# Strassen weight sums made by accumulating DMAs from GpSimd's queue in place of VectorE additions

## What is computed

```python
def lora_add(base, inp, A, B):                 # one A, B pair per sequence, rank 16, scale 0.5
    return base + einsum('bor,bnr->bno', B, einsum('bri,bni->bnr', A, inp)) * 0.5

# block 1: W_gate, W_up (1376, 512), W_down (512, 1376)
act  = silu(lora_add(x @ W_gate.T)) * lora_add(x @ W_up.T)
y    = lora_add(act @ W_down.T)
# block 2: RMS norm of y, gate_w, up_w (1792, 512), down_w (512, 1792)
nx   = y * rsqrt(mean(y * y) + 1e-5) * ln_w
out  = x + (silu(nx @ gate_w.T) * (nx @ up_w.T)) @ down_w.T
```

## Time and profile before

| | us |
|---|---|
| median of 3 runs | 397.09 (396.99 to 397.59) |
| span of the profiled execution | 395.5 |
| TensorE busy (matmuls) | 391.8 |
| VectorE busy | 314.8 |
| ScalarE busy | 240.8 |
| GpSimd busy | 10.6 |
| HBM read | 29.95 MB |

### The profile page before, as it was taken

One profiled execution on the slowest core, in us unless ns is written; L12 is line 12 of the kernel. 1 busy time (PEld: TensorE's weight loads), 2 busy tenths in 40 slices (PEclk: granted clock), 3 DMA queues, 4 the chain that ended last, 5 costly groups with the idle time before them and its releaser, 6 DMA issues.

```text
span 395.5 us, 5733 instructions
## 1 busy us (share of the span) xinstructions
PE 391.8 (99%) x1984; PEld 327.3 (83%) x1984; DVE 314.8 (80%) x476; ACT 240.8 (61%) x386; POOL 10.6 (3%) x13
## 2 busy tenths in 40 slices
PE   9999999999999999999999999999999999999997
PEld 5899888888888888888888888888888888888885
DVE  4899979586835869578699787878787869899994
ACT  5969786857574469815745656464646494484740
POOL 6300000000000000000000000000000000000000
PEclk9999999999999999999999999999999999999999
DMA  7640243311111551000400021313130316105112
GB/s 271 182 133 0 83 133 98 110 53 55 53 55 54 164 154 57 2 0 0 159 2 1 12 97 55 106 53 108 60 119 37 89 57 199 55 1 201 54 53 108
DMA packets 14942, 32.42 MB, mean 82 GB/s; under 512 B 2370, under 2 KB 4930, under 8 KB 14914
## 3 DMA queue, kind: packets, MB, share of 16 engines
q1 hardware_dynamic: 13792, 30.22, 23.7%
q10 hardware_dynamic: 1122, 1.84, 1.3%
HBM read 29.95 MB, written 2.10 MB: 81 GB/s over the span
## 4 chain that ended last, share of the span: by engine, by line
PE 99%; DVE 0%; issue 0%; DVEq 0%
PE bank L1365 53%; PE bank L1705 17%; PE bank L1593 14%; PE bank L1511 3%; PE bank L1557 3%; PE bank L1546 3%; PE bank L1375 3%; PE bank L1615 1%; PE bank L1607 1%; PE bank L1505 1%; PE bank L1714 0%; PE bank L1622 0%; DVE act L1354 0%; DVEq L1352 0%
## 5 line engine op out<-in xcount | busy, mean ns | idle before, releaser
L1365 PE MATMUL bank<-xs,ws 128*128 128x512 f32 x840 | 195.0, 390 | 0.0
L1365 PEld LDWEIGHTS bank<-xs,ws 128*128 128x128 f32 x840 | 156.6, 188 | 31.9
L415 ACT ACTIVATE xs<-act 128x512 fp32r<-128x512 f32 x71 | 42.8, 623 | 21.1 <-DVE act L1045 7.6
L1593 PE MATMUL bank<-xs,wdc 128*128 128x512 f32 x240 | 55.7, 390 | 0.0
L1593 PEld LDWEIGHTS bank<-xs,wdc 128*128 128x128 f32 x240 | 44.8, 188 | 9.5 <-issue 0.2
L889 DVE TENSOR_TENSOR xs<-act,xs 128x512 fp32r<-128x512 f32 x71 | 47.5, 685 | 2.7 <-ACT xs L415 2.1
L889 DVE TENSOR_TENSOR ws<-wraw,ws 128x256 fp32r<-128x256 f32 (+2 forms) x45 | 30.0, 668 | 13.0 <-ACT ws L415 12.8
L415 ACT ACTIVATE bank<-bank 128x512 f32<-128x512 f32 x30 | 17.3, 580 | 34.5 <-PE bank L1365 33.7
L415 ACT ACTIVATE mu<-bank 128x512 f32<-128x512 f32 x44 | 26.1, 596 | 20.1 <-PE bank L1365 13.6
L1705 PE MATMUL bank<-xs,vs 128*128 128x512 f32 x168 | 38.2, 389 | 0.0
L1705 PEld LDWEIGHTS bank<-xs,vs 128*128 128x128 f32 x168 | 31.5, 188 | 6.5
(11 more groups left out here) (133 smaller groups left out, 439.5 us busy)
## 6 DMA issues: line engine op xcount, KB each, us to landing
wraw<-wgu_in SPq DMA_DIRECT2D x22, 512.0 KB, 3.3
wdr<-vs_in SPq DMA_DIRECT2D x7, 512.0 KB, 3.6
wraw<-vj_in SPq DMA_DIRECT2D x3, 896.0 KB, 4.7
wdr<-wd_in SPq DMA_DIRECT2D x10, 256.0 KB, 2.7
xa<-xT_in SPq DMA_DIRECT2D x4, 256.0 KB, 4.1
xa<-xT_in ACTq DMA_DIRECT2D x2, 512.0 KB, 4.7
bgu_raw<-bgu_in SPq DMA_DIRECT2D x32, 32.0 KB, 1.9
xres<-xT_in SPq DMA_DIRECT2D x4, 256.0 KB, 3.5
```

The source lines that it names most:

```text
L415: return nc.scalar.activation(out_ap, in_ap, ACT.Copy, scale=scale)
L1365: ins = mm(z[:, :], w_slot(j)[:, w, s, k * P:(k + 1) * P], xs[:, c, r, k, :], start=(start and k == 0 and s == 0 and r == 0), stop=(k == 1 ...
L1593: ins = mm(z[:, :], wd[:, s, h * P:(h + 1) * P], x[r], start=(start and s == 0 and r == 0), stop=False, skip_group_check=True)
```

## The change

The host hands over the raw blocks of each weight set three times: `wgu_in` holds the three blocks that are split as they are (384 KB a set), `wbase_in` four blocks with which the sums begin (512 KB), and `wmore_in` three blocks that are added to the first three of these (384 KB). SyncE loads the first into `wraw` and the second straight into `wsum`, which has two buffers now. GpSimd then issues two DMAs that add to their destination: `wmore_in` onto blocks 0 to 2, and, when that has landed, block 1 onto blocks 2 and 3. `wraw` and `wsum` become parts of one tensor, `wbuf`; the order of two sums in the weight slot is swapped; the mask lies in memory that was free at that time; the zeroing of `ad` stands behind the sums of set 9. Steps 1, 3 and 4 above keep their places and waits, but for the semaphore on which `hi_b` waits.

```diff
-W11, W12, W22, WS3, WS1, WS2, WS4 = range(7)
+W11, W12, W22, WS3, WS1, WS4, WS2 = range(7)
...
-        mask = sb("mask", [P, CH], f32)
...
-        wraw = sb("wraw", [P, 2, 4, 256], f32)
-        wsum = sb("wsum", [P, 4, 256], f32)
+        wbuf = sb("wbuf", [P, 14, 256], f32)
...
             raw1 = sb("bgu_raw1", [P, 4, CHUNK[1]], f32, way)
+            sb("skip_ad", [P, 64], f32, way)
+            mask = sb("mask", [P, CH], f32, way)
...
-        w0_raw = wraw[:, :, :, :].rearrange("p a b n -> p (a b n)").rearrange("p (k x) -> p k x", k=KT)
+        wraw = wbuf[:, 0:6, :].rearrange("p (a b) n -> p a b n", a=2)
+        wsum = wbuf[:, 6:14, :].rearrange("p (a b) n -> p a b n", a=2)
+        w0_raw = wbuf[:, 6:14, :].rearrange("p b n -> p (b n)").rearrange("p (k x) -> p k x", k=KT)
...
-        jraw = wraw[:, :, :, :].rearrange("p a b n -> p (a b) n")
-        dm5 = wsum[:, :, :].rearrange("p a n -> p (a n)").rearrange("p (i n) -> p i n", i=2)
+        jraw = wbuf[:, 0:KF, :]
+        dm5 = wbuf[:, 10:14, :].rearrange("p a n -> p (a n)").rearrange("p (i n) -> p i n", i=2)
...
-                sp.dma_start(wraw[:, j % 2, :, :], wgu_in[j - 2].rearrange("p (a m) -> p a m", a=4)
+                sp.dma_start(wraw[:, j % 2, :, :], wgu_in[j - 2].rearrange("p (a m) -> p a m", a=3)
                              ).then_inc(s_w_ld[j % 2], 16)
+                sp.dma_start(wsum[:, j % 2, :, :], wbase_in[j - 2].rearrange("p (a m) -> p a m", a=4)
+                             ).then_inc(s_wbase_ld[j % 2], 16)
...
-            pool.wait_ge(s_stklo, 8)
-            nc.gpsimd.memset(ad[:, :, :, RANK:2 * RANK], 0.0).then_inc(s_ad_pad, 1)
+            for j in range(2, G2):
+                part = wsum[:, j % 2, :, :]
+                pool.wait_ge(s_wbase_ld[j % 2], 16 * (j // 2))
+                nc.gpsimd.dma_start(part[:, 0:3, :], wmore_in[j - 2].rearrange("p (a m) -> p a m", a=3), accum_op=ALU.add
+                                    ).then_inc(s_wsum1[j % 2], 16)
+                pool.wait_ge(s_wsum1[j % 2], 16 * (j // 2))
+                nc.gpsimd.dma_start(part[:, 2:4, :], part[:, 1:2, :].to_broadcast([P, 2, 256]), accum_op=ALU.add
+                                    ).then_inc(s_wsum2[j % 2], 16)
+                if j == G1 - 1:
+                    pool.wait_ge(s_stklo, 8)
+                    nc.gpsimd.memset(ad[:, :, :, RANK:2 * RANK], 0.0).then_inc(s_ad_pad, 1)
...
             def hi_b(j):
                 w_free(j)
-                a.wait_ge(s_wsum, 3 * (j - 2) + 3)
-                copy(w_slot(j - 2)[:, 3:7, 0, :], wsum[:, :, :]).then_inc(s_wbhi, 1)
+                a.wait_ge(s_wsum2[j % 2], 16 * (j // 2))
+                copy(w_slot(j - 2)[:, 3:7, 0, :], wsum[:, j % 2, :, :]).then_inc(s_wbhi, 1)
...
-            def sums(j):
-                g = j - 2
-                v.wait_ge(s_w_ld[j % 2], 16 * (j // 2))
-                if g >= 1:
-                    v.wait_ge(s_wbhi, w_of(g - 1) - 1)
-                    v.wait_ge(s_wblo, w_of(g - 1) - 1)
-                raw_w = wraw[:, j % 2, :, :]
-                nc.vector.tensor_tensor(wsum[:, 0:2, :], raw_w[:, 1::2, :], raw_w[:, 0:1, :].to_broadcast([P, 2, 256]),
-                                        ALU.add).then_inc(s_wsum, 1)
-                v.wait_ge(s_wsum, 3 * g + 1)
-                nc.vector.tensor_tensor(wsum[:, 2, :], wsum[:, 1, :], raw_w[:, 1, :], ALU.add).then_inc(s_wsum, 1)
-                v.wait_ge(s_wsum, 3 * g + 2)
-                nc.vector.tensor_tensor(wsum[:, 3, :], wsum[:, 2, :], raw_w[:, 2, :], ALU.add).then_inc(s_wsum, 1)
...
-                if w_next(j) < last:
-                    sums(w_of(w_next(j)))
...
+        "wgu_in": blocks_of(wgu, [1, 2, 3]),
+        "wbase_in": blocks_of(wgu, [1, 3, 2, 1]),
+        "wmore_in": blocks_of(wgu, [0, 0, 1]),
```

More of the change, by code:

```diff
@@ L42, with build @@
 RING_F = (X11, XT1, XT2, X21, X22, XT3, XT4)
-def build(nc, xT_in, idx_in, wsh_in, w0_in, wgu_in, wd_in, vs_in, vj_in, agu_in, bgu_in, ad_in, bd_in, lnw_in, out):
+def build(nc, xT_in, idx_in, wsh_in, w0_in, wgu_in, wbase_in, wmore_in, wd_in, vs_in, vj_in, agu_in, bgu_in, ad_in, bd_in, lnw_in, out):
     f32, f32r, i32 = mybir.dt.float32, mybir.dt.float32r, mybir.dt.int32
@@ L427, in hi_a @@
                 w_free(j)
-                copy(w_slot(j - 2)[:, 0:3, 0, :], wraw[:, j % 2, 1:4, :]).then_inc(s_wahi, 1)
+                copy(w_slot(j - 2)[:, 0:3, 0, :], wraw[:, j % 2, :, :]).then_inc(s_wahi, 1)
             def hi_b(j):
                 w_free(j)
-                a.wait_ge(s_wsum, 3 * (j - 2) + 3)
-                copy(w_slot(j - 2)[:, 3:7, 0, :], wsum[:, :, :]).then_inc(s_wbhi, 1)
+                a.wait_ge(s_wsum2[j % 2], 16 * (j // 2))
+                copy(w_slot(j - 2)[:, 3:7, 0, :], wsum[:, j % 2, :, :]).then_inc(s_wbhi, 1)
             def ca(j):
@@ L907, in lo_a @@
                 part = w_slot(j - 2)
-                sub(part[:, 0:3, 1, :], wraw[:, j % 2, 1:4, :], part[:, 0:3, 0, :]).then_inc(s_walo, 1)
+                sub(part[:, 0:3, 1, :], wraw[:, j % 2, :, :], part[:, 0:3, 0, :]).then_inc(s_walo, 1)
             def lo_b(j):
@@ L912, in lo_b @@
                 part = w_slot(j - 2)
-                sub(part[:, 3:7, 1, :], wsum[:, :, :], part[:, 3:7, 0, :]).then_inc(s_wblo, 1)
+                sub(part[:, 3:7, 1, :], wsum[:, j % 2, :, :], part[:, 3:7, 0, :]).then_inc(s_wblo, 1)
             def c12_begin(j):
@@ L1170, in _ @@
             short_act(0)
-            sums(2)
             x_sum(0, 2)
@@ L1770, in pairs, with blocks_of @@
         t = w.reshape(2 * apart, P, 2, 256 // P, P).transpose(0, 2, 4, 3, 1).reshape(2 * apart, 2, P, 256)
-        return np.stack([np.stack([t[i + apart, 0], t[i, 0], t[i, 1], t[i + apart, 1]], 1).reshape(P, 4 * 256)
-                         for i in range(apart)])
+        return np.stack([np.stack([t[i + apart, 0], t[i, 0], t[i, 1], t[i + apart, 1]], 1) for i in range(apart)])
     def groups(gate, up, apart):
-        return np.stack([pairs(gate, apart), pairs(up, apart)], 1).reshape(2 * apart, P, 4 * 256)
+        return np.stack([pairs(gate, apart), pairs(up, apart)], 1).reshape(2 * apart, P, 4, 256)
+    def blocks_of(w, which):
+        return w[:, :, which].reshape(w.shape[0], P, len(which) * 256)
     seq_b = [(0, 10), (1, 10)] + [(g, p + 5 * i) for p in range(5) for g in range(2) for i in range(2)]
@@ L1788 @@
     blocks = {(i, j): wd_f[j, :, :, i] for i in range(2) for j in range(2)}
+    wgu = np.concatenate([groups(wg[:NC * P], wu[:NC * P], NC // 2)[2:],
+                          groups(arr("L0_ffn_gate_w"), arr("L0_ffn_up_w"), NF // 2)], 0)
     feeds = {
@@ L1794 @@
             2, 2, P, KT, P).transpose(3, 4, 0, 1, 2).reshape(KT, P, 4 * P),
-        "wgu_in": np.concatenate([groups(wg[:NC * P], wu[:NC * P], NC // 2)[2:],
-                                  groups(arr("L0_ffn_gate_w"), arr("L0_ffn_up_w"), NF // 2)], 0),
+        "wgu_in": blocks_of(wgu, [1, 2, 3]),
+        "wbase_in": blocks_of(wgu, [1, 3, 2, 1]),
+        "wmore_in": blocks_of(wgu, [0, 0, 1]),
         "wd_in": wd_c,
```

7 lines of the change are left out of this document (3 added, 4 removed).

## The result

| version | median us | runs |
|---|---|---|
| before | 397.10 (396.52 to 397.67) | 20 |
| changed | 398.09 (397.30 to 399.22) | 20 |

The ratio is 1.0025, with a 95% interval of 1.0017 to 1.0034: the change makes the kernel 1.0 us slower. That lies inside the stated range, but it is 1.0 us above the forecast of 397.1, on the side to which 0.24 was given.

The account below looks back on a forecast made before the run. The prediction took TensorE, busy 391.8 of 395.5 us, to bound the kernel. Removed work, loads, accumulation pair and memset each counted 0, so span 395.5 and time 397.1 us, with a range of 396.6 to 402.0.

Parts of the forecast that it names:

- B: Rival: slower, the serial pair is too long and the wait for the sums replaces that for VectorE; chance 0.13.
- D: Rival: slower by a fixed sum for GpSimd's DMA queue set-up or drain at a kernel end, 398.7 us; chance 0.06.
- A: The forecast itself: the pair of accumulations is hidden behind matmuls, 397.1 us; chance 0.73.
- The bound, and the value of VectorE's 33.8 us: TensorE bounds the kernel; the removed VectorE additions lie beside matmuls, so their value on the path is 0.
- rival E: Faster: relief of VectorE or ScalarE lets TensorE start or end earlier, at most half a microsecond, 396.6 us; chance 0.03.
- Loads: First step added: SyncE's two transfers a set, bases landed 5.0 us after the first issue; cost 0.
- The pair: Second step: GpSimd's two serial accumulating DMAs, pair time x = 9.2 us, bounded by 5.8 and 17.3 us; cost 0.
- My own last part: List of signs for right or wrong; among them the FFN groups' DMA share rising from 22% to 40% or more.
- The start: The first set's sum, the tightest place: x may be 11.4 us; at 9.2 it is ready half a microsecond ahead.
- The slack in the groups: Third step: one set bears x = 14.0 us in FFN groups, 15.5 before; with repeated loads, loss starts at 12.2 and 14.2.
- the price curve: Rival B's times by pair time x: 402.1 us at 13, 407 at 14, 422.6 at 16, about 433 at 17.3.
- Rival C, the port: Slower: GpSimd's issues get through only in VectorE's idle 17%, 4.1 us each, x = 16.0, 422.6 us; chance 0.05.

Follow-up runs that it names:

- One add: Changed kernel without the second accumulation of each set, so two of the four sums lack a term; 397.23 us (0.9998).
- the second trace: The changed kernel run again with no edit, for another trace; 397.94 us (1.0019).
- Set 2 early: Changed kernel with the load of weight set 2 issued ahead of the second half of the first LoRA stacks; 397.78 us (1.0013).
- three adds: Changed kernel with the second accumulation cut in two DMAs, the second waiting for the first; 418.62 us (1.0524).

## Why the prediction was off by 1 us

The time lies in the range, and the limits that the prediction set for a set's sum were nearly right; the term that went into them, the pair time, was not. By its own signs this is a mild form of B (a hole near 40 us and pairs above 11.4 us) together with a small fixed part as in D, and not A: the chain is 89% PE and not 99%, and from a set's load to its sum it took 13.5 to 21.1 us where 12 to 16 was put.

**The bound, and the value of VectorE's 33.8 us: right.** "One add" frees the same time and stands at 397.23. The kernel has no hole for a gain to show in, so rival E has fallen as well.

**Loads: right in the median.** 5.0 us from the first issue to the bases' landing were taken. Their landing after their own issue (0.37 us later), and the others (KB each, median us):

```profile
...
wbuf<-wbase_in SPq DMA_DIRECT2D x22, 512.0 KB, 4.9
wbuf<-wgu_in SPq DMA_DIRECT2D x22, 384.0 KB, 3.3
wbuf<-wmore_in POOLq DMA_DIRECT2D x22, 384.0 KB, 5.1
wbuf<-wbuf POOLq DMA_DIRECT2D x22, 256.0 KB, 4.1
```

That is 5.3 us in the median, from 4.2 to 7.5 us over the sets, and set 2's bases were there at 24.59 where 24.9 was put.

**The pair: right alone, wrong in company. This is the step that failed.** GpSimd's two groups, with the time of the issue in ns and the landing in us (min/median/max):

```profile
...
L418 POOL DMA_DIRECT2D wbuf<-wmore_in x22: 914/924/1471, 24.9 to 301.4; - x22
...
DMA to landing us min/median/max: 4.6/5.1/7.8
```

```profile
...
L421 POOL DMA_DIRECT2D wbuf<-wbuf x22: 1200/1214/1230, 33.0 to 306.7; - x22
...
DMA to landing us min/median/max: 3.6/4.1/7.7
```

I had 5.0 us for the first with its issue and 4.2 for the second. The smallest landings are 4.6 and 3.6, and with 0.35 and 0.4 us for GpSimd to see a landing, a set with nothing beside it (the last one) has a pair time of 9.3 us for my 9.2. But the medians are higher and the maxima 7.8 and 7.7 us: over the sets, the pair took 9.3 to 14.0 us, 10.9 in the median. The step that failed is the sentence that the DMA engines are 22% busy, so crowding is unlikely. I read the share of the kernel before, while the change itself takes the bytes a set from 512 KB to 1536 KB. The same windows after (busy us (count) of PE, PEld, DVE, ACT, POOL; PEclk, DMA share, GB/s):

```profile
...
41.00:124.00 83.00, 82.87 (x398) 69.67 (x399) 50.14 (x59) 59.45 (x90) 17.49 (x18) 1.00 0.77 178
...
192.00:325.00 133.00, 133.00 (x591) 110.15 (x590) 96.00 (x134) 74.66 (x116) 21.38 (x20) 1.00 0.61 150
```

61% in the FFN groups, where it was 22%, and 77% in the groups before, where it was 26%:

```profile
...
41.00:124.00 83.00, 83.00 (x398) 69.76 (x397) 59.59 (x80) 58.69 (x91) 0.70 (x1) 1.00 0.26 79
```

My own last part said "40% or more" and drew nothing from it. Set 6 shows what that does: GpSimd issues its second accumulation at 73.20, just when SyncE has sent the 896 KB of set 7.

```profile
...
72.23 0.33 SPq L286 DMA_DIRECT2D wbuf<-wgu_in  x1
72.60 0.43 SPq L288 DMA_DIRECT2D wbuf<-wbase_in  x1
```

GpSimd, this issue and that of the last set, which has no load beside it:

```profile
...
73.20 1.20 POOL L421 DMA_DIRECT2D wbuf<-wbuf  x1 [4.79 <-DMA wbuf<-wmore_in]
...
306.74 1.22 POOL L421 DMA_DIRECT2D wbuf<-wbuf  x1 [4.42 <-DMA wbuf<-wmore_in]
```

The last set's sum lands 3.6 us after this issue, set 6's 7.7 us, and ScalarE, waiting, goes on at 80.99:

```profile
...
80.99 1.06 ACT L430 ACTIVATE ws<-wbuf 128x1024 fp32r<-128x1024 f32 x1 [1.88 <-DMA wbuf<-wbuf]
```

There is a second lengthening that the prediction had left out: GpSimd serves the sets one after the other. The 14.0 us are those of set 15, whose bases had landed at 201.33 while GpSimd was still waiting for set 14's pair:

```profile
...
205.08 1.22 POOL L421 DMA_DIRECT2D wbuf<-wbuf  x1 [4.66 <-DMA wbuf<-wmore_in]
205.78 1.47 POOL L418 DMA_DIRECT2D wbuf<-wmore_in  x1
```

That cost nothing here, since nobody asked for this sum yet. The longest pair made by crowding alone is that of set 6, 13.7 us.

The Trainium skill, page "DMA: Bandwidth & Descriptors", section "Issuing engines are not separate DMA queues", says that transfers of all issuing engines run on the same 16 DMA engines and interleave; this trace agrees, with 3.6 us for a second accumulation alone and 7.7 us for one beside a load. The same page, section "Anatomy of one DMA — SWDGE (gpsimd) path", fits 2.0 us + bytes / 436e3 to a DMA from GpSimd, by which these sizes would take an estimated 2.9 and 2.6 us; the accumulating ones measured here never took less than 4.5 (in the second trace) and 3.6.

**The start: the place was right, and the limit within half a microsecond.** The limit for set 2 was a pair time of 11.4 us; it was 12.01, the loss put at 12.01 - 11.4 = 0.6 us, and TensorE's gap there is 0.45 us longer than usual. "Set 2 early" removed it. In the second trace of the changed kernel the pair took 11.27 us, under the limit, and TensorE still lost 0.3 us: when the bases land and when TensorE gets there differ from one execution to the next, and the limit with them. The error that counts is that 9.2 us stood in the sum, while the small loads and set 3's load were known to be in flight there.

**The slack in the groups was put 1.1 us too large.** In both kinds of groups I let the split end when g_prod starts. But VectorE has more behind it, here for set 6:

```profile
...
82.08 1.22 DVE L904 TENSOR_TENSOR ws<-wbuf,ws 128x1024 fp32r<-128x1024 f32 x1 [2.64 <-ACT ws L430]
83.22 0.68 DVE L961 TENSOR_TENSOR act<-act,bank 128x512 f32<-128x512 f32 x1
83.82 0.68 DVE L920 TENSOR_TENSOR mu<-mu,bank 128x512 f32<-128x512 f32 x1
84.53 0.69 DVE L933 TENSOR_TENSOR act<-act,mu 128x512 f32<-128x512 f32 x1
85.14 0.68 DVE L945 TENSOR_TENSOR mu<-mu,bank 128x512 f32<-128x512 f32 x1
```

Four instructions follow the split of the sums, and the last, `c22_sum`, is wanted by product p4, one product after g_prod. From the end of the split to the end of `c22_sum` it is 85.82 - 83.30 = 2.5 us, and from g_prod's start to p4's 1.36 us: the split must end 1.1 us sooner than I took. I had written what stands behind ScalarE's wait and not what stands behind VectorE's, which inherits the wait. TensorE's holes at 86 us (first trace, 0.1 us) and 270 us ("set 2 early", 0.5 us) are of this kind.

**Rival B, the price curve.** The mechanism and its place were right, and the curve is borne out at its far end: "three adds", with 13.5 to 17.6 us, cost 21.4 us and stands at 418.6, between my 407 (x = 14) and 422.6 (x = 16). That the two meet is partly luck: about 3 us of the cost is the lower clock, which the curve does not have, and part of the 13.5 to 17.6 us is GpSimd still being busy with the set before.

**Rival C, the port: refuted.** GpSimd's issues took 914 to 940 ns (1039 the first) and 1200 to 1230 ns throughout, while VectorE was 96 of 133 us busy; the only longer ones (1.45 to 1.47 us) are first accumulations issued straight behind a second one. Rival C had 4.1 us. The Trainium skill, page "SBUF — State Buffer", section "Who interferes with whom", says that `tensor_tensor` has no two-port mode; the trace agrees in so far as no issue got longer beside VectorE's work, which is mostly of this form.

**Rival D, a fixed cost: wrong in its cause, right that one exists.** The queue costs nothing (1.76 us outside the span), and there is no later first matmul or longer tail in the trace. But 0.35 of the 1.0 us lies outside the span, with the 22 accumulations whose source has a step of zero. No view shows where in the execution it lies. The whole time around the span, which I had put at 1.6 us from one span and a median of other runs, is 1.74 us in 33 runs of the kernel before.

Together: 0.35 us outside, shown to go with that one form of DMA. Inside, about 0.6 us in the medians of the span; it goes with the second accumulation ("one add"), and the first trace, 0.9 us longer than that of the kernel before from matmul 58 on, has about 0.6 us of holes behind late sums. In the versions whose traces have no such hole the median span is still 0.2 to 0.3 us above that of the kernel before beside them. Whether other executions of theirs have late sums, or something else is at work, stays open.

## What to carry to other kernels

When work moves to DMAs, take the DMA engines' share after the change, not before it, and price a chain of transfers both alone and beside each transfer that can be in flight. For a wait that moves, write down what is queued behind it on each engine that it passes through, the waiting engine's successor as well. When a delay makes holes in TensorE's work, look at the granted clock behind them as well. And a bound of a fixed cost needs the time outside the span of several runs of each version: it stayed within 1.73 to 1.79 us in all versions without that form of DMA, and here it told apart a cost that no trace shows.

## What was not expected of the hardware

An accumulating DMA from DRAM to SBUF of 384 KB landed in 4.6 us at best (4.5 in the second trace), one of 256 KB within SBUF in 3.6; GpSimd is busy 0.92 and 1.21 us with their issue, also in the stages where VectorE is busy 72% of the time. A second accumulation that reads one block twice, 22 times in a kernel, goes with 0.35 us more outside the span (2.09 to 2.14 against 1.73 to 1.79); two plain ones in its place don't, and a single one in the last set doesn't either. That it grows with their number is only a guess. The granted clock fell to 0.50 for 3 to 4 us behind two of the holes of "three adds", and not behind a third of 2.4 us at 292 us. The start of TensorE's matmul 58 differed by 0.5 us between traces of the kernel before and by 0.7 between two of the changed one. The runs of the changed kernel spread wider (397.3 to 399.2) than those of the kernel before (396.5 to 397.7); late sums, which differ from one execution to the next, are a likely reason, not a shown one.
